# Two norms before one feed-forward: the second norm's rows turned by VectorE through a DRAM scratch

## What is computed

```python
ga = (2 * (ga >= 0) - 1) * maximum(abs(ga), 0.25)      # gb the same
h = layernorm(x) * (1 + ca) + sa
x = x + ga * (h @ w.T + bias)                          # w: weight, masked in 32x32 blocks, 1024x1024
h = layernorm(x) * (1 + cb) + sb
g, u = h @ (gate_w * gate_s).T, h @ (up_w * up_s).T    # 2752 x 1024 each
x = x + gb * ((silu(g) * u) @ (down_w * down_s).T)
```

## Time and profile before

| | us |
|---|---|
| median of 3 runs | 1124.59 |
| lowest, highest | 1124.07, 1126.71 |
| the profiled execution, its own time | 1126.06 |
| span of the profiled execution | 1124.3 |

### The profile page before, as it was taken

One profiled execution on the slowest core, in us unless ns is written; L12 is line 12 of the kernel. 1 busy time (PEld: TensorE's weight loads), 2 busy tenths in 40 slices (PEclk: granted clock), 3 DMA queues, 4 the chain that ended last, 5 costly groups with the idle time before them and its releaser, 6 DMA issues. The chain is left out here.

```text
span 1124.3 us, 13245 instructions
## 1 busy us (share of the span) xinstructions
PE 1089.5 (97%) x4741; PEld 509.9 (45%) x4741; DVE 739.7 (66%) x926; ACT 428.7 (38%) x783; POOL 375.0 (33%) x346
## 2 busy tenths in 40 slices
PE   4899999999999999999999999999999899999998
PEld 1544454555444444444444444444444344444444
DVE  2739367767678898888797888879545343334434
ACT  1332236656556455445555555555432000000000
POOL 1105237546655353315655564655200000000000
PEclk8699999999999999999999999999999999999999
DMA  9993212426353555446666665675288665565431
GB/s 342 404 387 83 75 40 73 113 57 203 125 197 103 166 173 177 116 126 195 183 206 192 188 180 175 194 198 178 76 345 333 235 245 230 218 245 220 184 144 38
DMA packets 130001, 206.94 MB, mean 184 GB/s; under 512 B 20624, under 2 KB 99216, under 8 KB 127504
## 3 DMA queue, kind: packets, MB, share of 16 engines
q1 hardware_dynamic: 124640, 184.08, 49.8%
q0 software_dynamic: 5296, 22.02, 5.5%
HBM read 137.39 MB, written 68.68 MB: 183 GB/s over the span
## 5 line engine op out<-in xcount | busy, mean ns | idle before, releaser
L1302 PE MATMUL pA<-work 128*128 128x512 f16 x1680 | 377.0, 379 | 4.6 <-ACT work L1043 2.9
L1302 PEld LDWEIGHTS pA<-work 128*128 128x128 f16 x1680 | 163.7, 98 | 205.1 <-ACT work L1043 6.0
L1166 PE MATMUL pA<-work 128*128 128x512 f32 x512 | 225.0, 593 | 0.0
L1302 PE MATMUL pB<-work 128*128 128x512 f16 x752 | 175.9, 379 | 1.4 <-DVE work L1700 1.4
L1166 PEld LDWEIGHTS pA<-work 128*128 128x128 f32 x512 | 95.0, 190 | 112.3 <-issue 111.4
L1722 DVE SCALAR_TENSOR_TENSOR work<-work 128x512 f16<-128x512 f16 x144 | 122.8, 875 | 19.2 <-ACT work L1063 19.0
L1369 PE MATMUL pA<-work 128*128 128x512 f16 x600 | 134.4, 379 | 0.0
L913 ACT ACTIVATE work<-pB,small 128x128 f32<-128x128 f32 x256 | 92.6, 477 | 72.2 <-PE pB L1155 60.9
L1043 ACT ACTIVATE work<-pA 128x512 f32<-128x512 f32 x126 | 74.6, 592 | 116.4 <-PE pA L1302 111.2
L1302 PEld LDWEIGHTS pB<-work 128*128 128x128 f16 x752 | 73.5, 98 | 90.1 <-DVE work L1700 2.1
L1369 PE MATMUL pB<-work 128*128 128x512 f16 x480 | 109.0, 383 | 3.3 <-DMA work<-h_left_scratch 3.3
(11 more groups left out here) (170 smaller groups left out, 1067.7 us busy)
## 6 DMA issues: line engine op xcount, KB each, us to landing
work<-h_scratch SPq DMA_DIRECT2D x8, 4480.0 KB, 13.7
h_scratch<-work SPq DMA_DIRECT2D x60, 512.0 KB, 3.1
work<-in_L_wmod SPq DMA_DIRECT2D x10, 2048.0 KB, 16.2
work<-in_L_ffn_gate_w SPq DMA_DIRECT2D x84, 128.0 KB, 3.3
work<-in_L_ffn_up_w SPq DMA_DIRECT2D x84, 128.0 KB, 2.9
work<-down_scratch SPq DMA_DIRECT2D x7, 1280.0 KB, 11.5
work<-in_L_ffn_down_w SPq DMA_DIRECT2D x68, 128.0 KB, 2.8
work<-in_L_attn_data SPq DMA_DIRECT2D x16, 512.0 KB, 4.4
```

The source lines that it names most:

```text
L1166: last = pe.matmul(pA[:, 2 * par(t) + h, :], hT1[par(t)][:, c, :], wT[:, c, h * H:(h + 1) * H], start=(c == 0), stop=(c == KT - 1))
L1302: last = pe.matmul(ps, w[:, m, c], bc[b][:, mv_, s, c], start=begin, stop=(i == n - 1 and c == KT // 2 - 1 and s == 1), skip_group_check=True)
```

## The change

TensorE no longer turns the second norm's blocks. `normalise(1, t)` writes `z2` in its natural order; SyncE stores it to a DRAM scratch (512 KB) and loads it back into one buffer `zb` in four DMAs of 128 KB, with the 32x32 squares already at the right places; VectorE turns the squares into PSUM with one instruction. There is one `z2`, one `zb` and one PSUM target: `normalise(1, t)` waits for the store of block `t - 1` to land, `load_zb(t)` for `turn(t - 1)`, and `turn(t)` for the four loads and for `second_input(t - 1)`.

The row `ga` is multiplied into `wT` once (`scale_rows`, eight instructions of 128x1024 on VectorE), so that `residual(t)` of blocks 2 to 15 is one addition from PSUM in place of a product and an addition. The row sums 4 and 5 and `gate_row(2)` move ahead of `attend(0, 1)` on TensorE. The buffers of the row sums change places to free `gbs` for `zb`.

```diff
+            def store_z(t):
+                sp.wait_ge(z_done[1], t + 1)
+                sp.dma_start(z_d[t], z2).then_inc(z_stored, 16)
+
+            def load_zb(t):
+                sp.wait_ge(z_stored, 16 * (t + 1))
+                if t == 0:
+                    sp.wait_ge(acc_used, 5)
+                else:
+                    sp.wait_ge(t_done[1], t)
+                for a in range(A):
+                    sp.dma_start(zb[Q * a:Q * (a + 1)].rearrange("p (b k) -> p b k", b=A), z_v[t, a])\
+                      .then_inc(zb_loaded, 16)
...
+                if t in (3, 4):
+                    store_z(t - 3)
+                if t == 5:
+                    load_zb(0)
+                    store_z(2)
+                    load_zb(1)
+                if t in FIRST:
+                    store_z(FIRST[t] + 2)
+                    load_zb(FIRST[t] + 1)
+                if t >= 10:
+                    store_z(t - 1)
+                    load_zb(t - 1)
+                if t in SECOND:
+                    if t < 9:
+                        store_z(SECOND[t] + 2)
+                    load_zb(SECOND[t] + 1)
...
                     elif t >= 4:
-                        pe.wait_ge(pair_free, t - 3)
+                        pe.wait_ge(x1_ready, t - 1)
+                if t == 2 and ks[0] == 0:
+                    pe.wait_ge(w_scaled, 4 * h + 4)
...
-                if t in MID:
-                    transpose(1, MID[t])
...
-                if t in END:
-                    transpose(1, END[t])
...
-                if g == 1:
-                    transpose(1, LAST)
...
+            def turn(t):
+                dve.wait_ge(zb_loaded, 16 * A * (t + 1))
+                if t >= 1:
+                    dve.wait_ge(hf_ready, t)
+                else:
+                    dve.wait_ge(row_copied, 10)
+                dst = z2T.rearrange("p h n -> p (h n)")
+                dve.transpose(dst.rearrange("p (c b i) -> p c b i", c=KT, b=A),
+                              zb.rearrange("p (b c i) -> p c b i", b=A, c=KT)).then_inc(t_done[1], 1)
+
+            def scale_rows(h):
+                if h:
+                    dve.wait_ge(attn_done, 2)
+                else:
+                    dve.wait_ge(acc_used, 3)
+                row = ga[:, H * h:H * (h + 1)].rearrange("p (o n) -> p o n", o=1).to_broadcast([P, 2, H])
+                for c in range(0, KT, 2):
+                    w = wT[:, c:c + 2, H * h:H * (h + 1)]
+                    dve.tensor_tensor(w, w, row, ALU.mult).then_inc(w_scaled, 1)
...
-                dve.tensor_tensor(x1_of(t), ps, ga, ALU.mult).then_inc(pair_free, 1)
-                dve.wait_ge(pair_free, t - 1)
-                finish(t)
+                dve.wait_ge(xg_ready, t + 1)
+                dve.tensor_tensor(x1_of(t), ps, xg[par(t)], ALU.add).then_inc(x1_ready, 1)
...
+            turn(0)
+            normalise(1, 2)
             residual(5)
             for t in range(6, NT + 1):
+                if t >= 10:
+                    turn(t - 2)
                 if t <= LAST - 2:
                     stats1(t + 2)
+                if t in FIRST:
+                    turn(FIRST[t])
+                    normalise(1, FIRST[t] + 2)
+                if 10 <= t <= LAST:
+                    normalise(1, t - 1)
...
+                if t in SECOND:
+                    turn(SECOND[t])
+                    if t < 9:
+                        normalise(1, SECOND[t] + 2)
...
                 if g == 1:
+                    turn(LAST)
                     lo_part(LAST - 1)
```

More of the change, by code:

```diff
@@ L214, in adaln_kernel @@
         blk1 = at(o + 4 * D, 4 * P)
[L215 removed]
+        acc = [acc_a, x1[0], acc_a, hf[0], gbs, gbs]
+        zb = gbs
         x1_late = [late[:, D * k:D * (k + 1)] for k in range(4)]
@@ L320, in adaln_kernel @@
         z_done = [sem(f"z_done{k}") for k in range(2)]
+        z_stored = sem("z_stored")
+        zb_loaded = sem("zb_loaded")
+        w_scaled = sem("w_scaled")
         t_done = [sem(f"t_done{k}") for k in range(2)]
@@ L465, in value_of @@
             return up[m == A22]
-        MID = {3: 0, 6: 1, 7: 3, 8: 5, 9: 6, **{t: t - 2 for t in range(10, NT + 1)}}
-        END = {6: 2, 7: 4, 9: 7}
+        FIRST = {6: 1, 7: 3, 8: 5, 9: 6}
+        SECOND = {6: 2, 7: 4, 9: 7}
         SUMS_AT = {6: 1, 7: 3, 8: 5, 10: 7, **{t: t - 2 for t in range(11, LAST + 1, 2)}}
@@ L941, in _ @@
                 move_row_half(u)
-            copy_row(4)
-            copy_row(5)
+                if u == 13:
+                    copy_row(4)
+                    copy_row(5)
             def second_input(r):
@@ L1147, in _, with transpose @@
         def _(pe):
-            def transpose(L, t):
-                z, dst, taken = ((z1, z1T, hT1_ready), (z2, z2T, hf_ready))[L]
-                zc = z.rearrange("p (c k) -> p c k", c=KT)
-                pe.wait_ge(z_done[L], t + 1)
+            def transpose(t):
+                zc = z1.rearrange("p (c k) -> p c k", c=KT)
+                pe.wait_ge(z_done[0], t + 1)
                 if t >= 1:
-                    pe.wait_ge(taken, t)
+                    pe.wait_ge(hT1_ready, t)
                 for c in range(KT):
-                    last = pe.transpose(dst[:, c // 4, (c % 4) * P:(c % 4 + 1) * P], zc[:, c], ident)
-                last.then_inc(t_done[L], 1)
+                    last = pe.transpose(z1T[:, c // 4, (c % 4) * P:(c % 4 + 1) * P], zc[:, c], ident)
+                last.then_inc(t_done[0], 1)
             def attend(t, h, ks=range(KT)):
@@ L1224, in _ @@
             pe.wait_ge(consts_set, NCONST)
-            transpose(0, 0)
+            transpose(0)
             pe.wait_ge(silu_c_done, 1)
@@ L1233, in _ @@
                 turn_rows(n)
-            transpose(0, 1)
+            transpose(1)
             pe.wait_ge(wT_by_dve, 4)
@@ L1242, in _ @@
                 attend(1, 0, range(2 * n - 10, 2 * n - 8))
+                if n == KT - 1:
+                    pe.wait_ge(mask_bits, 2)
+                    pe.wait_ge(cols1_ready, 2)
+                    row_sum(4)
+                    row_sum(5)
                 turn_rows(n)
@@ L1245, in _ @@
             pe.wait_ge(wT_ready, 2 * KT - 4)
-            pe.wait_ge(mask_bits, 2)
-            pe.wait_ge(cols1_ready, 2)
-            attend(0, 1, range(4))
-            row_sum(4)
-            row_sum(5)
-            attend(0, 1, range(4, KT))
             gate_row(2, rowp[0])
-            transpose(0, 2)
+            attend(0, 1)
+            transpose(2)
             attend(1, 1)
@@ L1266, in _ @@
                 if t <= LAST - 1:
-                    transpose(0, t + 1)
+                    transpose(t + 1)
                 if t == 2:
@@ L1473, in normalise @@
                 dve.wait_ge(rstd_done[L], t + 1)
-                if t >= 1:
-                    dve.wait_ge(t_done[L], t)
-                if L:
-                    z = z.rearrange("p (c a i) -> p a c i", c=KT, a=A)
-                    src = src.rearrange("p (a c i) -> p a c i", c=KT, a=A)
-                dve.tensor_scalar(z, src, mv[L][place(t)][:, 0:1], rstd[L][place(t)], ALU.subtract, ALU.mult).then_inc(z_done[L], 1)
+                if L == 0 and t >= 1:
+                    dve.wait_ge(t_done[0], t)
+                elif t >= 1:
+                    dve.wait_ge(z_stored, 16 * t)
+                dve.tensor_scalar(z, src, mv[L][place(t)][:, 0:1], rstd[L][place(t)], ALU.subtract, ALU.mult).then_inc(z_done[L], 1)
+            def turn(t):
+                dve.wait_ge(zb_loaded, 16 * A * (t + 1))
+                if t >= 1:
+                    dve.wait_ge(hf_ready, t)
[13 more added lines that the diff above has]
+                    dve.tensor_tensor(w, w, row, ALU.mult).then_inc(w_scaled, 1)
             def stats1(t):
@@ L1488, in norm1 @@
                 normalise(0, t)
-            def finish(t):
-                dve.wait_ge(xg_ready, t + 1)
-                dve.tensor_tensor(x1_of(t), x1_of(t), xg[par(t)], ALU.add).then_inc(x1_ready, 1)
-                dve.wait_ge(x1_ready, t + 1)
-                stats(1, t, x1_of(t))
             def residual(t):
@@ L1510, in residual_of_evacuated @@
                 link(dve.tensor_tensor(x1[t], x1[t], ga, ALU.mult))
-                finish(t)
+                dve.wait_ge(xg_ready, t + 1)
+                dve.tensor_tensor(x1[t], x1[t], xg[t], ALU.add).then_inc(x1_ready, 1)
+                dve.wait_ge(x1_ready, t + 1)
+                stats(1, t, x1[t])
             def turn_unit(u):
@@ L1652, in _ @@
             gate_a()
+            scale_rows(0)
             normalise(0, 3)
             residual_of_evacuated(0)
+            scale_rows(1)
             normalise(1, 0)
@@ L1687, in _ @@
                     normalise(0, t + 2)
-                if t in MID and t > 3 and t <= LAST:
-                    normalise(1, MID[t] + 1)
                 if t <= LAST:
                     residual(t)
-                if t in END:
-                    normalise(1, END[t] + 1)
+                if t in SECOND:
```

(3 more changed lines are left out.)

16 lines of the change are left out of this document (8 added, 8 removed).

## The result

| | before | after |
|---|---|---|
| median, us | 1124.93 | 1135.55 |
| lowest, highest | 1124.07, 1126.71 | 1135.31, 1140.86 |
| runs | 4 | 4 |
| span of the profiled execution | 1124.3 | 1133.7 |
| its own time | 1126.06 | 1135.56 |

The changed kernel is slower: the ratio is 1.0106, 95% interval 1.0091 to 1.0122. The forecast was 1127.4 with a range of 1119 to 1134. The time lies 1.6 us beyond the upper end, and the direction, slower by more than 0.3%, was not that of the forecast.

What follows compares the result with a forecast made beforehand. TensorE, busy 97% of the span, was taken as the bound, just hiding a three-engine loop. Terms -13.9 - 1.7 + 0.9 + 15.1 + 1.2 + 1.2 = +2.8 us gave 1128.9 profiled, median 1127.4; range 1119 to 1134.

Steps and rivals of the forecast that it cites:

- The walk's waits: TensorE's waits, found by walking the new program order with profiled durations: 2.8, 0.8, 3.0, 7.4 and 1.1, together +15.1 us.
- the loop through sums(7): At block 12: turn(8)'s reload delays stats1(12), then GpSimd's sums(7), lo_part(7) and the norm TensorE wants; 7.4 us.
- The reload: Bringing a block back into zb: 3.6 to 7.5 us possible, 5.3 taken, since only a store stands ahead.
- the prediction's signs of being wrong: Block 12's first transpose before 240, turn(8) not waiting for the reload, or waits in iterations 12 to 15.
- Scaling the weights: Eight VectorE products before attention end 2, delaying `attend(2, 0)` and `attend(2, 1)`: +0.9 us, bounds 0 to 3.
- The turn into PSUM: VectorE's instruction per block, taken as 1.2 us, 2 at most, never waiting for GpSimd.
- the term of the clock: Half-speed work behind the 7.4 us wait: 2.3 us, less the 1.1 wait it fills, so +1.2.
- The end of the stage: Unit 6 loads late behind store_z(15) and load_zb(15), so TensorE waits longer for `up2` of group 1: +1.2 us (0 to 3).
- Full gain: First rival: TensorE stays the bound and the whole gain arrives, -14.7 us, 1109.9; chance 0.07.
- the quick reload: Second rival: reloads take 3.6 us and the clock is kept, -2.9 to -5.0 us, 1119.6 at the latter; chance 0.13.
- the third, the slow reload: Reloads take 7.5 us, three costing 2.2 more each, +9.4 us, 1134.0; chance 0.44, including walk's hand-offs adding up.

Runs made afterwards that it cites:

- e3: Changed kernel with idle identity products on TensorE, 4 ahead of `attend(9, 0)` and 9 ahead of the transpose of block 12; 1133.56 us, ratio to before 1.0087.
- e8: Changed kernel with `scale_rows(0)` issued ahead of the bias product on VectorE, before GpSimd's two additions; 1135.56 us, ratio to before 1.0098.
- e5: Changed kernel without scaled weights: the residual is again a product with ga and an addition; 1139.19 us, ratio to before 1.0128.
- e2: Changed kernel with two zb buffers, so a block's reload waits for turn(t - 2), not turn(t - 1); 1132.58 us, ratio to before 1.0083.
- e1: Changed kernel with stats1(t + 2) ahead of turn(t - 2) on VectorE in iterations 10 to 13; 1130.56 us, ratio to before 1.0055.
- e7: Changed kernel with four repairs together (e1, e2, e6, e8); 1123.92 us, ratio to before 0.9988.
- e6: Changed kernel with SyncE loading weight units 6 and 7 ahead of the store and reload of block 15; 1130.52 us, ratio to before 1.0055.
- e12: Changed kernel with the 32 one-column instructions split, half in `attend(5, 0)` and half in `attend(5, 1)`; 1133.80 us, ratio to before 1.0089.
- e10: e9 with the 32 one-column instructions split, half in `attend(5, 0)` and half in `attend(5, 1)`; 1121.07 us, ratio to before 0.9972.
- e9: e7 with turn_out(9) ahead of hi_part(3) and (4), turn_out(11) ahead of cast_unit(0) on ScalarE, and lo_part(3) after turn(5) on VectorE; 1124.28 us, ratio 1.0001.
- e4: Kernel before with scaled weights, one-instruction residual and moved row sums, transposes kept on TensorE; 1125.32 us, ratio to before 1.0007.

## Why the prediction was off

**What held.** The 128 transposes and the wait at 191.47 went, at -13.9 and -1.7. The walk's waits were forecast as 2.8, 0.8 and 3.0 ahead of `attend(9, 0)`, (10, 0) and (11, 0), 7.4 at the transpose of block 12 and 1.1 behind it, 15.1 in all. Measured were 4.3, 0, 0.5, 8.8 and 0, with 0.3 ahead of `attend(8, 0)`: 13.9. The two longest are where the walk has its queues: turn_out(9) behind second_input(4) and the hi parts, and the loop through sums(7). That at (11, 0) was 3.0 in the walk and 0.5 here; TensorE came to it later, by 1.5 us more of wait and 2.9 of half clock at (9, 0), and in e3, where the clock stayed, it was 2.89. VectorE's waits ahead of turn(4), (7) and (8) were to be 1, 2 and 4 us and were 0.9, 2.1 and 5.0. The reload took 6.1 and not 5.3. None of the prediction's signs of being wrong came. Scaling the weights cost 1.5 (0.9, with 3 as the bound), and no wait came in iterations 12 to 15. The turn into PSUM took 1.26 us, also at 232.08, where GpSimd's addition (230.90 to 233.25) was under way. The rule cited from the Trainium skill (SBUF — State Buffer, Who interferes with whom) held for the products of e8, 4.63 us alone and 8.94 beside GpSimd; the same section puts `tensor_scalar` in its two-port mode among those that contend, which the prediction left out and the norm of 2.94 us in e8, against 0.81, agrees with.

**The step that failed** is the term of the clock: "I take 2.3 [...] less the 1.1 us wait behind it that it fills: +1.2". It counts one fall, behind the 7.4 us wait. That one cost 2.4, and no later wait was there for it to fill. But the level fell at four places, for 8.7 us: also behind 4.28 and 2.99 us, and once behind work of one column. The prediction had a level kept after 1.67 us and low after 10.10, and its own waits of 2.8 and 3.0, and of 2.6 in group 1 (1.36 and 1.2 more), lay between the two; it priced the falls behind them at nothing. That 2.3 came so near to 2.4 is partly luck: its bound is taken from the low level behind a gap at 42.71, but the level was low ahead of that gap already, TensorE's timeline of before (8 transposes at the upper level take 1.04 to 1.09):

```profile
39.86 1.97 PE L1221 MATMUL pA<-ident,work 128*128 128x128 f32 x8 [1.64 <-DVE work L493]
```

**Not each fall lengthens the run.** The prediction says that a half clock fills a wait behind it, and the runs show this at `attend(9, 0)` (all runs that turn the second norm on VectorE with ScalarE's order as in after, but e5 with its slower residual):

| | `attend(9, 0)` takes | wait ahead of `attend(11, 0)` | from the start of the one to that of the other |
|---|---|---|---|
| after | 10.01 | 0.50 | 32.87 |
| e2 | 9.61 | 1.16 | 33.12 |
| e1 | 8.83 | 1.98 | 33.16 |
| e8 | 8.76 | 2.05 | 33.16 |
| e7 | 8.62 | 2.55 | 33.52 |
| e6 | 8.60 | 2.14 | 33.09 |
| e12 | 8.57 | 2.19 | 33.11 |
| e3 | 7.13 | 2.89 | 33.33 |

The attend takes up to 2.9 us less, and `attend(11, 0)` starts no sooner for it: it waits for ScalarE's turn_out(11). So the fall at 207 took the place of waits that the walk had (0.8 and most of 3.0), and pricing it alone would have added next to nothing. Beside the one at block 12, which the forecast has, two falls had no wait behind them to fill, and these are what the forecast lacks: 1.7 us behind the columns (without it, e12 starts group 0 1.3 sooner) and 1.7 us in group 1 (gone in e6 together with its wait).

**Terms mis-sized.** The end of the stage was to cost 1.2 us and cost 2.7. Its cause was named rightly, unit 6 behind store_z(15) and load_zb(15), and e6 shows it; the hand-off was another. The prediction has `third(1)` wait longer for VectorE's `up2`, but that wait was 1.06 us (353.92). The one that grew, 2.99, is for ScalarE's L1079, which stands behind the cast of unit 6. The waits at (9, 0) and at the transpose of block 12 were 1.5 and 1.4 us longer than walked, with reloads that took 0.8 more each.

Measured less forecast: start of the run -2.0, prologue +0.6, (8, 0) +0.3, (9, 0) +1.5, the fall there with the waits at (10, 0) and (11, 0) -0.4 (3.4 against 3.8), block 12 +1.4, what stands behind it +0.1 (2.4 against 1.1 and 1.2), the columns' fall +1.7, the end of the stage +1.5, the fall in group 1 +1.7. That makes 6.4 of the 6.6 us between +2.8 and +9.4. The medians lie 8.1 us from the forecast, since it took off the 1.5 us by which the profiled execution of before lay above its median, and that of after lay on its own (1135.56, 1135.55).

**The rivals.** Full gain and the quick reload are out. The time is nearest to that of the third, the slow reload at 1134.0, but its mechanism is not what happened: the reloads cost about 0.8 each more than taken, not 2.2, and two zb gave back 3 us of a wait of 8.76. Since this case had the larger chance (0.44 against 0.36), a forecast on its side would have been nearer for a reason that was only half right.

**Where the gain went.** e10 shows it best: TensorE is busy for 14.4 us less than before (1075.1 against 1089.5), and 10.6 us of waits up to group 0 take most of that back. TensorE at 97% hid a loop of VectorE, GpSimd and ScalarE that in iterations 6 to 10, where the second norm catches up, is nearly as slow as TensorE was. e2 and e9 each opened the next wait behind the one they closed. Whether more of the 13.9 us comes when the catching up is spread over more iterations was not tried.

**Open:** why the times of e4, e7 and e9 spread by 7 to 10 us and those of e10 by 3.5. The length of the low level in the prologue differs between profiled executions, and waits of the same length are sometimes followed by the low level and sometimes not; that both together make the spread is only argued.

## What to carry to other kernels

Work taken off the bounding engine is worth its duration only up to the next loop's period: walk the other engines' programs in order, and where the walk gives waits, price the half clock behind each of them, not behind the longest alone, and then ask whether a wait behind it swallows it: in this kernel only the falls with no wait to fill lengthened the run. When a wait is found, look at the order of the queue in which the late instruction stands: moving two lines on VectorE gave back 5 us where a second buffer gave 3 (by the medians), and moving the loads on SyncE as much. A repair that shows nothing in the time (e8) may still have closed its wait: here a longer low level at another place took the gain, and one execution can't tell that from the edit.

## What was not expected of the hardware

- TensorE fell to 1.2 GHz without any wait, behind 32 instructions of one column in which the profile has it busy throughout (3.7 us in after; window 148 to 152: busy 4.00 of 4.00, clock 0.57). It did so in 7 of 11 profiled executions with the 32 together (not in those of before, e2, e3 and e9), and in none of three with 16 and 16. That the columns are the cause rests on these counts.
- A wait of the same length goes both ways. Over all fourteen profiled executions, from 70 to 400 us, none of 20 waits of TensorE of 1.2 to 1.86 us was followed by durations of the lower level, 8 of 13 waits of 1.87 to 2.28 were, and all 24 of 2.47 and more. In e10 an attend behind 2.03 us took 7.13, in e8 one behind 2.05 took 8.83. The Trainium skill (TensorE: Matmul & The Clock Gate, Part 1) has the slow level as the default that idleness brings back, and the rows of waits agree; the fall behind the columns came without idleness that the profile shows.
- A fall behind a wait slows float32 products by 1.4 to 2.9 us (8.57 to 10.01 us for an attend in place of 7.13), that at the columns by 1.7 to 3.4 (3.4 in e8: 4.67, 1.95 and 5.05 us for 3.63, 1.07 and 3.60). The size does not follow the wait: 1.7 behind 1.98 to 2.23 us, 1.4 behind 4.50, 2.9 behind 4.28, 2.4 behind 8.76.
